# One product for router logits and low-rank factors, and the folded keys moved beside the folded values

## What is computed

```
xn = layernorm(x)                                   # [8, 256, 128]
s  = attention(xn, w_q, w_k, w_v, w_o)              # 1024 wide, scaled by 1/32, causal
logits = xn @ gate_w.T + gate_b                     # 8 experts
top_v, top_i = top_k(softmax(logits), 2)
for e in range(8):
    gate  = (top_i == e).sum(-1) * top_v.sum(-1)
    inter = xn @ wi.T + bi + (xn @ lora_A[e].T) @ lora_B[e].T   # rank 16 of each expert
    out  += gate * (relu(inter) @ wo.T + bo)
x = x + s * silu(out)
...                                                 # second layer: 16-head differential attention, 32 experts of 64
```

## Time and profile before

| what | value |
|---|---|
| median of 3 runs | 491.97 us (491.80 to 492.65) |
| the profiled execution | 493.67 us, of which the span of the core is 491.9 us |
| TensorE busy | 93% of the span |
| VectorE busy | 81% |
| ScalarE busy | 57% |
| GpSimd busy | 55% |

### The profile page before, as it was taken

One profiled execution on the slowest core, in us unless ns is written; L12 is line 12 of the kernel. 1 busy time (PEld: TensorE's weight loads), 2 busy tenths in 40 slices (PEclk: granted clock), 3 DMA queues, 4 the chain that ended last, 5 costly groups with the idle time before them and its releaser, 6 DMA issues.

```text
span 491.9 us, 8510 instructions
## 1 busy us (share of the span) xinstructions
PE 455.2 (93%) x3072; PEld 219.5 (45%) x3072; DVE 398.6 (81%) x812; ACT 281.6 (57%) x456; POOL 269.6 (55%) x237
## 2 busy tenths in 40 slices
PE   2999888889999999999999999999889998989995
PEld 2755447434444345453454444544334453423332
DVE  1634457999998988899999978978999999986785
ACT  2264673446767635738876445556776537467640
POOL 6322360235554775547763459636675865546982
PEclk9999997999999999999999999999999999999998
DMA  7900059786952710232569643025592662204201
GB/s 277 338 14 0 22 182 194 127 142 182 234 111 76 127 18 4 73 84 65 176 181 168 111 62 91 1 65 171 178 172 43 121 98 77 58 5 113 59 2 43
DMA packets 54754, 52.44 MB, mean 107 GB/s; under 512 B 5080, under 2 KB 44344, under 8 KB 54072
## 3 DMA queue, kind: packets, MB, share of 16 engines
q1 hardware_dynamic: 54712, 51.90, 44.2%
HBM read 37.47 MB, written 13.89 MB: 104 GB/s over the span
## 4 chain that ended last, share of the span: by engine, by line
PE 73%; DVE 18%; ACT 3%; issue 2%; POOLq 1%; DMA 1%; POOL 1%; SPq 0%; DVEq 0%; ACTq 0%
PE bank L785 10%; PE bank L776 9%; PE bank L797 8%; PE scores L816 8%; PE bank L871 5%; DVE nmax L1335 3%; PE scores L711 3%; PE scores L702 3%; PE scores L726 3%; PE scores L705 3%; PE scores L810 3%; PE scores L750 3%; DVE h L1311 3%; PE bank L876 2%; DVE h L1318 2%
## 5 line engine op out<-in xcount | busy, mean ns | idle before, releaser
L1136 POOL TENSOR_TENSOR gb<-gb,wb 128x512 f32<-128x512 f32 x64 | 84.3, 1318 | 94.3 <-ACT gb L1024 76.3
L1039 ACT ACTIVATE pk<-scores 128x1024 f32<-128x1024 f32 x96 | 95.3, 1023 | 38.9 <-PE scores L816 38.7
L1129 POOL TENSOR_SCALAR_AFFINE_SELECT pk<-pk 128x512 f32<-128x512 f32 (+1 forms) x96 | 82.1, 864 | 39.8 <-ACT pk L1039 39.3
L1335 DVE TENSOR_REDUCE nmax<-scores 128x8 f32<-128x1024 f32 x64 | 76.4, 1216 | 7.7 <-PE scores L816 7.0
L1021 ACT ACTIVATE gt<-bank,bgh 128x512 f32<-128x512 f32 (+1 forms) x68 | 46.7, 687 | 62.5 <-PE bank L776 50.7
L785 PE MATMUL bank<-xnt,wu 128*128 128x512 f32 x128 | 68.3, 615 | 2.3 <-DVE h L1318 2.2
L776 PE MATMUL bank<-xnt,wg 128*128 128x512 f32 x128 | 69.4, 624 | 0.0
L797 PE MATMUL bank<-h,wd 128*128 128x512 f32 x128 | 66.5, 617 | 0.0
L1311 DVE SCALAR_TENSOR_TENSOR h<-gt,gb 128x512 f32<-128x512 f32 x64 | 57.8, 903 | 3.4 <-PE bank L797 3.1
L1318 DVE SCALAR_TENSOR_TENSOR h<-bank,bu,h 128x512 f32<-128x512 f32 x64 | 48.1, 751 | 10.8 <-PE bank L785 8.8
L1140 POOL TENSOR_TENSOR orms<-oms,minus_half 128x32 f32<-128x32 f32 x8 | 44.7, 5585 | 10.3 <-DVE oms L1365 10.3
(11 more groups left out here) (262 smaller groups left out, 711.1 us busy)
## 6 DMA issues: line engine op xcount, KB each, us to landing
wb<-wt_scratch SPq DMA_DIRECT2D x64, 256.0 KB, 4.2
parts_scratch<-parts SPq DMA_DIRECT2D x16, 384.0 KB, 3.0
qa<-parts_scratch SPq DMA_DIRECT2D x32, 192.0 KB, 4.9
ka<-parts_scratch SPq DMA_DIRECT2D x32, 192.0 KB, 5.9
parts_scratch<-parts SPq DMA_DIRECT2D x16, 256.0 KB, 3.1
parts_scratch<-parts SPq DMA_DIRECT2D x16, 128.0 KB, 2.8
ha<-in_wkq SPq DMA_DIRECT2D x1, 1024.0 KB, 4.8
wb<-in_wvo SPq DMA_DIRECT2D x1, 1024.0 KB, 7.5
```

What stands on the lines that cost most here:

```text
L1039: A(dst.rearrange("p (h m) q -> p m h q", m=2), pairs[pair_of(step)][:, :, :].rearrange("p m (h q) -> p m h q", q=cols), ACT.Exp, scale=SC ...
L1129: pool.affine_select(out=dst, in_=dst, compare_op=ALU.is_ge, fill=0.0, base=0, pattern=[[0, heads], [1, P]], channel_multiplier=-1).then_i ...
L1136: pw(gb[:, c % 2, :], gb[:, c % 2, :], wb[:, k % 2, j % 2, :], ALU.mult).then_inc(s_ga_done, 1)
L1335: V.tensor_reduce(dst, src, AX, ALU.max, negate=True).then_inc(s_nmax_done, 1)
```

## The change

The low-rank factors and the gate weights become one tile `lag` of 136 columns. One product for each tile of tokens gives both; it is made in step keys0 and fills parts of both banks of that step's pair. The folded keys' product and its copy move into step inner0, ahead of the folded values. The pair of keys0 is therefore free only when VectorE has made `um` (semaphore um_done), and that of inner0 when `yk` and `vw` have been copied. In chunk 0 both foldings are made in step inner0, one behind the other. Loads, sizes and PROGRAM are unchanged.

```diff
-        la = sb("la", [P, E0 * R0])
+        lag = sb("lag", [P, E0 * R0 + E0])
+        la, gate_w = lag[:, 0:E0 * R0], lag[:, E0 * R0:]
-        gate_w = sb("gate_w", [P, E0])
...
+        def inner(c):
+
+            return pairs[pair_of(("keys0", c))][:, :, :].rearrange("p n (k s) -> p (n k) s", s=2 * P)
...
             elif kind == "keys0":
+                pe.wait_ge(s_um_done, at(c, "um_done", 2))
+            elif kind == "inner0":
                 pe.wait_ge(s_yk_sb, at(c, "yk_sb", 1))
-                pe.wait_ge(s_lsub, at(c, "lsub", 1))
-            elif kind == "inner0":
                 pe.wait_ge(s_vw_sb, at(c, "vw_sb", 1))
-                pe.wait_ge(s_um_done, at(c, "um_done", 2))
...
                     for k in range(TILES):
-                        last = mm(two[:, k * E0:(k + 1) * E0], xnt_of[side(c)][:, k * P:(k + 1) * P], gate_w[:, :], start=(k == 0), stop=True, skip_group_check=True)
+                        last = mm(inner(c)[:, k, 0:E0 * R0 + E0], xnt_of[side(c)][:, k * P:(k + 1) * P], lag[:, :],
+                                  start=(k % 2 == 0), stop=True, skip_group_check=True)
                     last.then_inc(s_logits_ps, 1)
+                elif name == "inner0":
+
                     if c == 0:
                         pe.wait_ge(s_kq_in, 16)
                         fold(4, kq_room, s_mt_done)
+                        pe.wait_ge(s_vo_in, 16)
+                        fold(5, vo_room, s_vo_done)
                         pe.wait_ge(s_mt_copied, 1)
                     mm(one, mt[:, :], xnt_of[side(c)][:, :], start=True, stop=True).then_inc(s_yk_ps, 1)
-                elif name == "inner0":
-
-                    for k in range(TILES):
-                        last = mm(one[:, k * P:(k + 1) * P], xnt_of[side(c)][:, k * P:(k + 1) * P], la[:, :], start=(k == 0), stop=True, skip_group_check=True)
-                    last.then_inc(s_u_ps, 1)
                     if c == 0:
-                        pe.wait_ge(s_vo_in, 16)
-                        fold(5, vo_room, s_vo_done)
                         pe.wait_ge(s_vo_copied, 1)
...
-                elif name == "keys0":
+                elif name == "router0":
+                    act.wait_ge(s_lsub, at(c, "lsub", 1))
+                    A(lexp_of[side(c)][:, :, :], lexp_of[side(c)][:, :, :], ACT.Exp).then_inc(s_lexp_done, 1)
+                elif name == "inner0":
                     if c == 0:
                         act.wait_ge(s_mt_done, 1)
                         A(mt[:, :], bank[4][:, 0:P], ACT.Copy).then_inc(s_mt_copied, 1)
                     act.wait_ge(s_yk_ps, at(c, "yk_ps", 1))
                     A(yk_of[side(c)][:, :], pairs[pair][:, 0, :], ACT.Copy).then_inc(s_yk_sb, 1)
-                elif name == "router0":
-                    act.wait_ge(s_lsub, at(c, "lsub", 1))
-                    A(lexp_of[side(c)][:, :, :], lexp_of[side(c)][:, :, :], ACT.Exp).then_inc(s_lexp_done, 1)
-                elif name == "inner0":
...
-                    dve.wait_ge(s_u_ps, at(c, "u_ps", 1))
                     for j in range(2):
-                        V.tensor_tensor(um_of[side(c)][:, j, :, :].rearrange("p c (e r) -> p (c e) r", r=R0),
-                                        one.rearrange("p (g r) -> p g r", r=R0),
-                                        wide(pick_of[side(c)][:, j, :, :].rearrange("p c e -> p (c e)"), R0), ALU.mult).then_inc(s_um_done, 1)
+                        V.tensor_tensor(um_of[side(c)][:, j, :, :].rearrange("p c (e r) -> p c e r", r=R0),
+                                        inner(c)[:, :, 0:E0 * R0].rearrange("p c (e r) -> p c e r", r=R0),
+                                        pick_of[side(c)][:, j, :, :].unsqueeze(3).to_broadcast([P, TILES, E0, R0]), ALU.mult).then_inc(s_um_done, 1)
```

More of the change, by code:

```diff
@@ L343, in build @@
         s_logits_ps = sem("logits_ps")
-        s_u_ps = sem("u_ps")
         s_lsub = sem("lsub")
@@ L422, in build @@
         PER = dict(x_in=16, var0=1, rstd0=1, xn0=TILES, xnt_ps=1, xnt_sb=1, yk_ps=1, yk_sb=1, vw_ps=1, vw_sb=1,
-                   s0_ps=CB, nb0=1, p0_done=TILES, pt_ps=CB, pt_sb=CB, att_ps=1, logits_ps=1, u_ps=1, lsub=1,
+                   s0_ps=CB, nb0=1, p0_done=TILES, pt_ps=CB, pt_sb=CB, att_ps=1, logits_ps=1, lsub=1,
                    lexp_done=1, um_done=2, umt_ps=2, umt_sb=2, inter_ps=FB, inter2_ps=FB, ha_done=FB, hb_done=FB,
@@ L1206, in front @@
                     dve.wait_ge(s_logits_ps, at(c, "logits_ps", 1))
-                    link(V.tensor_tensor(logit_of[side(c)][:, :, :], two[:, 0:TILES * E0].rearrange("p (c e) -> p c e", e=E0),
+                    link(V.tensor_tensor(logit_of[side(c)][:, :, :], inner(c)[:, :, E0 * R0:E0 * R0 + E0],
                                          gate_b[:, :].unsqueeze(1).to_broadcast([P, TILES, E0]), ALU.add))
```

## The result

The changed kernel takes 500.66 us in the median of 6 runs (498.73 to 502.87); the kernel before, timed beside it, 492.31 us (491.53 to 493.16, 6 runs). The ratio is 1.0169, with a 95% interval of 1.0142 to 1.0196: 8.35 us slower. The profiled execution took 500.45 us (span 498.7 us), against 493.67 us (span 491.9 us) before: 6.8 us between the two traces.

What follows compares the result with a forecast made beforehand. TensorE (93% busy, 73% of the last-ending chain) was taken as the bound unless VectorE sets the pace. -0.6 + 1.2 - 0.8 + 4.1 + 3.2 = +7.1, less 0.8, gave +6.3: 498.3 us, range 494.8 to 501.0.

Steps and rivals of the forecast that it cites:

- The merged product: Logits and factors in one product: at most 0.95 us for 8 matmuls, saving TensorE 0.75 to 0.79 us per chunk.
- Chunk 0, forecast -0.6: Foldings back to back: the values' product starts at 20.5, not 21.16, so -0.6 us; bounds -1.2 and 0.
- The fast pace begins with the factors' product at 17.95: Chunk 0: matmuls run at half pace at first, so the second folding would end near 18.7 us.
- Chunk 1, forecast +1.2: TensorE pauses 2.1 us for `um` ahead of L702, which starts at 36.4, not 35.20: +1.2 us; bounds +1.1, +1.8.
- rival 2: The 2.1 us pause in chunk 1 brings the clock down too: another 3.2 us, 501.5 us; chance 0.07.
- Chunk 2, forecast -0.8: values1/0 starts at 82.0, not 83.10, and L810 near 84.1, not 84.93: -0.8 us; bounds -1.3 and -0.3.
- At half clock all is slower on TensorE alone: Chunk 2: TensorE runs at the lower clock there, so `um` isn't late; values1/0 starts at 82.0, not 83.10.
- Chunk 3, forecast +4.1 and a pause of 5.0: inner0/3: the keys' product waits 5.0 us for `um`, values start at 257.0, not 252.87: +4.1 us; bounds +3.3, +4.7.
- rival 3: Chunk 3's pause is given back later, VectorE's or GpSimd's backlog being the real bound: 492.5 to 494 us; chance 0.08.
- The 0.8 us taken off the sum: After chunk 3's pause, a late TensorE fills some of its 0.65 us idle time in the next 12 us: 0.8 off.
- The clock in chunk 3, forecast +3.2: Behind the 5.0 us pause the granted clock falls to 0.50 for one stretch: +3.2 us; bounds 0 and +3.9.
- the rule quoted in the prediction: A pause counts if the monitor sees the array idle; it costs half the throttled time: 6.4 us x 0.5 = 3.2.

Runs made afterwards that it cites:

- unmerged: The changed kernel's order and waits, but with the logits' and factors' products made apart in keys0; 501.62 us, 1.0202 against the kernel before.
- only0: The kernel before with the changed form in chunk 0 alone; 493.02 us, 1.0015 against the kernel before.
- only1: The kernel before with the changed form in chunk 1 alone; 498.56 us, 1.0120 against the kernel before.
- before_wait: The kernel before with one wait added: in inner0/3 TensorE waits for VectorE's up/24 ahead of the factors' product; 496.87 us, 1.0072.
- not3: The changed form in chunks 0, 1 and 2, the form of before in chunk 3; 494.26 us, 1.0048 against the kernel before.
- fill3: The changed kernel with ten zero matmuls on TensorE ahead of the wait in inner0/3; 499.35 us, 1.0154 against the kernel before.
- after_2: The changed kernel, nothing altered, profiled a second time; this execution took 507.09 us.
- only3: The kernel before with the changed form in chunk 3 alone; 498.83 us, 1.0128 against the kernel before.

## Why the prediction was right, and where it was off

The forecast was 498.3 us, 6.3 above the kernel before; measured were 500.66, 8.35 above. Sign, place and mechanism were right. Against the profiled execution, 6.8 us longer, the sum of 6.3 is 0.5 off, but only because terms that were off cancel; that closeness is luck.

- **The merged product.** 0.93 us for eight matmuls, forecast at most 0.95. `um` 1.29 us as taken. Right. That the saved work brings little by itself was right too: unmerged is 0.6 us slower.
- **Chunk 0, forecast -0.6.** Measured -2.1 at L665 (only0: -1.8). The change's own part is -1.0, inside the forecast's bounds. The other 1.1 us lie in the step "The fast pace begins with the factors' product at 17.95": it took for a property of the program what belonged to that execution. The same code came to its fast pace at 15.87 or earlier in only1, and in the kernel after the second folding ran all 16 matmuls fast, in 1.95 us from 15.37 on. The wait for `vo` behind `yk` is there, 0.85 us.
- **Chunk 1, forecast +1.2.** Measured 4.72 - 3.53 = 1.2 us at L702 for a pause of 1.88 us, 1.3 by chunk 2. Right. But rival 2, to which I gave 0.07, happened, though at half its price: the clock fell at 35.7 and 35.0 in the two executions of the kernel after and at 35.7 in only1, for 3.4 us and another 1.7 us of time. The argument against it, that TensorE is busy on both sides, was no argument.
- **Chunk 2, forecast -0.8.** The step "At half clock all is slower on TensorE alone" took for granted a fall that two executions of the kernel before have and that of only0 doesn't. Here the merged product ran at full clock, TensorE stood for 2.08 us ahead of L754, and the clock fell afterwards. From the logits to L810 it takes 84.92 - 77.27 = 7.65 us, 8.54 before: -0.9 by that count, but by luck. At full clock L810 stands 6.67 us behind the logits with the form of before (only0), 7.31 in before_wait, and 7.74 with the changed form (not3), so the change makes it later and the clock made it earlier. By chunk 3's logits little of either is left: -0.5 us against before, -0.3 for not3 (170.40) against only0 (170.71).
- **Chunk 3, forecast +4.1 and a pause of 5.0.** Measured 4.3 in fill3, and a pause of 4.85. Right, and before_wait shows that such lateness passes on to the end whole. That it would be given back (rival 3) is refuted for this place.
- **The 0.8 us taken off the sum.** They were to be filled by idle time in the next 12 us. The rows show nothing of the kind: with fill3 4.26 us of lateness at the values' product became 4.3 at the end, with before_wait 3.2 became 3.2.
- **The clock in chunk 3, forecast +3.2.** It fell, as forecast, but in the profiled execution at 254.1, inside the pause, so that only 4.4 us of it lay on work: about 2.1 us. In after_2 and only3 6.0 us lay on work: rears of 252.8, less 244.3, 4.3 for the pause and 1.3 for a second stretch, leave 2.9. The 3.2 us were read in chunk 2, as what TensorE loses on the spot; there only 0.5 of them was left at chunk 3, here all of it was. At this place the trace thus agrees with the rule quoted in the prediction (the Trainium skill, "TensorE: Matmul & The Clock Gate", section "HAM oscillation — how this bites in real kernels") on the price, about half the throttled time that lies on work (2.1 us of 4.4). The clock fell inside or behind every pause of 4.0 us and more (four traces), and stayed up in fill3 where the pause was filled, and in before_wait behind 2.93 us. But it also fell behind 1.88 us in three traces of seven, and before at 76.0, within a pause of 1.52 us.
- **The sum.** In the traces the terms are -2.1 (chunk 0), +3.0 (chunk 1), -0.5 (chunk 2), +4.3 and +2.1 (chunk 3): 6.8, against -0.6, +1.2, -0.8, +4.1, +3.2 and the 0.8 taken off. The forecast had too little gain in chunk 0 and too little loss in chunk 1. For the medians 2 us are missing, and 1.6 of them come from which executions were profiled: that of the kernel before was 1.4 us above its median, that of the kernel after 0.2 below. Charging every new pause of about 2 us with a short stretch would be too much, since the clock fell behind the one in chunk 1 in three traces of seven. In how many of the runs each stretch occurs can't be told from one trace for each kernel; the time at the lower level can, and its median is 16 us after and 7 us before.

## What to carry to other kernels

Where engines work through fixed lists and share buffers in a ring, look first at who frees the buffer that a merged product fills. To put two results into one buffer ties its next use to the slower reader of the two, and a saved product of 0.8 us can turn into a wait of 5. Ask what the reader's engine has in its list at that moment: the wait cost 4.3 us where VectorE stood 3 us behind TensorE, and 1.3 us in chunk 1 where only its own chain had to be waited for, each without the clock. With other steps moved in between, chunks 0 to 2 in the new form came out 3.1 us faster. On a kernel that TensorE bounds, a new pause costs its own length and then again the clock that it may take away; look for other products to fill it with before shortening the work. And before a term of a sum is read off one trace, see whether the clock in it belongs to the program or to that execution.

## What the runs showed of the hardware

- The clock falls behind pauses of 1.9 us in some executions (three traces of seven) and not behind 2.9 us in another. With the same code in front, chunk 3's logits' product came between 247.1 us (before_wait) and 249.7 us (only3), by where the slow stretches fell.
- The stretches at 0.50 come in two lengths in these traces, about 3.4 and about 6.8 us, the last one of each trace left out. Their price depends on the place: 1.3 us (not3, 439.2) and 1.7 us (after, 35.7) for the first, 0.5 us (before, 76.0), 2.7 us (only1, 441.9) and 4.7 us (after_2, 106.7) for the second. In a pause of TensorE the lower level costs less: 2.1 us with 2.4 of 6.8 us in the pause (after), 2.9 us with 0.8 (after_2). The kernel after has runs near 498.7, 500.6 and 502.8 us, steps of about 2 us.
- A float32 matmul with 8 columns is hardly cheaper than one with 136: 0.81 us and 0.93 us for eight.
- VectorE reads rows of 136 columns out of two banks at the speed of one plain bank, 1.29 us for 2 times 512 elements.
- Ten float32 matmuls with a matrix of zeros, 4.46 us, kept the granted clock at 1.00 where it fell without them (fill3 against after).
